# Expert stages begun in the tail of their attention, and keys, values and first queries of three attentions made in the stage before, in a four-layer transformer kernel

## The reference

```python
for i in range(4):
    x = x + attention_i(layernorm(x), ctx)     # a0, a1, a2, a3
    x = x + ffn_i(layernorm(x))                # f0, f1, f2, f3
```

```python
sel = sigmoid(x @ expert_sel.T)                # rows x 16
val, idx = top_k(sel, 4)
val = val / clip(val.sum(-1), 1e-9) * route_scale
out = sum_k val_k * (relu(x @ keys[idx_k]) @ values[idx_k])
```

## Time and profile before

| | us |
|---|---|
| median of 3 runs | 1240.81 (1240.06 to 1242.52) |
| the profiled execution | 1240.38 |
| its span | 1238.6 |
| mean granted TensorE clock, share of full | 0.926 |
| PE busy | 1009.9 (82%) |
| DVE busy | 906.6 (73%) |
| ACT busy | 618.2 (50%) |
| POOL busy | 354.7 (29%) |

### The profile page before, as it was taken

The page is one execution under the profiler, slowest core; times in us unless marked ns, Lnnn a source line. Parts: engine busy times, 40 slices in busy tenths (PEclk is TensorE's granted clock), DMA queues, the critical chain, the costliest instruction groups (busy, mean ns, idle before and its releaser), DMA issues.

```text
span 1238.6 us, 21285 instructions
## 1 busy us (share of the span) xinstructions
PE 1009.9 (82%) x7331; PEld 650.9 (53%) x7331; DVE 906.6 (73%) x2264; ACT 618.2 (50%) x966; POOL 354.7 (29%) x339
## 2 busy tenths in 40 slices
PE   5868700778978996899569999999789879999998
PEld 3653300734546773444227677776545446666665
DVE  4686699777875656778578898885678756666666
ACT  3424576356632335664277777765476423333332
POOL 5600000011210004354198999993111200000000
PEclk9889955789998999999769999999999979999999
DMA  7000000010000000000000000000000000000000
GB/s 272 1 1 1 1 0 0 1 65 1 2 2 1 0 1 1 2 2 2 1 1 2 1 0 0 0 0 1 1 2 2 2 0 10 8 8 8 8 9 18
DMA packets 8956, 13.47 MB, mean 11 GB/s; under 512 B 816, under 2 KB 6704, under 8 KB 8624
## 3 DMA queue, kind: packets, MB, share of 16 engines
q1 hardware_dynamic: 8880, 12.46, 2.9%
HBM read 10.36 MB, written 2.10 MB: 10 GB/s over the span
## 4 chain that ended last, share of the span: by engine, by line
PE 49%; DVE 31%; issue 10%; ACT 6%; POOL 2%; DVEq 1%; DMA 0%; SPq 0%; ACTq 0%; POOLq 0%
DVE big L718 7%; DVE big L713 6%; PE psum L511 5%; PE psum L1895 5%; PE psum L1898 5%; PE psum L1909 5%; DVE big L1802 2%; PE psum L1366 2%; PE psum L1319 2%; PE psum L252 2%; PE psum L1563 2%; PE psum L1328 2%; PE psum L1571 2%; DVE amax L1129 2%; PE psum L465 2%
## 5 line engine op out<-in xcount | busy, mean ns | idle before, releaser
L713 DVE TENSOR_REDUCE big<-psum 128x16 f32<-128x1024 f32 x96 | 114.4, 1221 | 70.4 <-PE psum L465 37.3
L1712 POOL TENSOR_TENSOR big<-big 128x512 f32<-128x512 f32 x128 | 128.7, 1047 | 21.5 <-ACT big L1632 21.5
L1945 ACT ACTIVATE big<-psum 128x512 f32<-128x512 f32 x80 | 47.8, 597 | 142.7 <-PE psum L1895 142.4
L383 POOL TENSOR_TENSOR big<-big,w_const 128x256 f32<-128x256 f32 x48 | 34.7, 724 | 229.4 <-PE psum L511 215.7
L1655 ACT ACTIVATE psum<-big,tmp 128x512 f32<-128x512 f32 x128 | 85.0, 687 | 22.7 <-DVE big L1802 20.0
L1802 DVE SCALAR_TENSOR_TENSOR big<-big,tmp,psum 128x512 f32<-128x512 f32 x128 | 90.4, 744 | 4.8 <-ACT psum L1655 1.9
L718 DVE RECIPROCAL big<-psum 128x256 f32<-128x256 f32 x48 | 84.0, 1750 | 13.4 <-PE psum L511 13.4
L1998 DVE TENSOR_TENSOR big<-big,psum 128x512 f32<-128x512 f32 x80 | 54.5, 687 | 52.6 <-PE psum L1898 52.3
L1909 PEld LDWEIGHTS psum<-tmp,big 128*128 128x128 f32 x512 | 66.7, 191 | 39.9 <-issue 36.3
L619 ACT ACTIVATE big<-psum 128x1024 f32<-128x1024 f32 x64 | 62.0, 1021 | 50.5 <-PE psum L495 50.5
L1328 PE MATMUL psum<-f_downT,tmp 128*128 128x128 f32 x192 | 24.6, 297 | 75.7 <-DVE tmp L1243 75.7
(11 more groups left out here) (241 smaller groups left out, 2319.1 us busy)
## 6 DMA issues: line engine op xcount, KB each, us to landing
out<-X SPq DMA_DIRECT2D x8, 256.0 KB, 2.3
tmp<-in_pack_f SPq DMA_DIRECT2D x1, 1924.0 KB, 7.7
w_f<-in_pack_f SPq DMA_DIRECT2D x1, 1280.0 KB, 12.1
tmp<-in_pack_once SPq DMA_DIRECT2D x1, 960.0 KB, 7.0
X<-in_x SPq DMA_DIRECT2D x1, 768.0 KB, 5.1
w_a<-in_pack_a SPq DMA_DIRECT2D x3, 256.0 KB, 7.5
w_a<-in_pack_a SPq DMA_DIRECT2D x1, 704.0 KB, 9.5
w_f<-in_pack_f SPq DMA_DIRECT2D x1, 576.0 KB, 5.0
```

Source lines behind the costliest of these rows:

```text
L713: dve.tensor_reduce(nm, psum[:, 1 + 2 * t:3 + 2 * t, :].rearrange("p c (r l k) -> p (c r) l k", r=2, k=SK), AX.X, ALU.max, negate=True).th ...
L1712: ins = pool.tensor_tensor(ssum[t][:, h * 512:(h + 1) * 512].rearrange("p (i j) -> p i j", i=ROWS2), st[:, 0, h, 0:ROWS2].unsqueeze(2).to_ ...
```

## The change

1. **Layer norm in parts.** The norms of a1, a2, a3, f1 and f3 are finished in two parts, the first over 16, 20, 20, 24 and 24 tiles. `ln_finish_dve` is split in `ln_var_dve` and `ln_rstd_dve`, and `normalise_act` lets ScalarE normalise a group (four activations).
2. **a1 in f0, a2 in f1, a3 in f2.** K and V of a1 stand ahead of f0's down products, the taking of keys (now eight ScalarE activations with a bias from a new `bk4`), values and keys16 in front of ScalarE's down levels; T, Q, MX and NM of batches 0 and 1 stand between the half groups of f0's groups 5 to 7 and behind them. a2's keys are made in f1's groups 1 to 4, its values in 5 and 6, T(0), Q(0) and Q(1) in 7. a3's all stand in f2's last group. All keys are complete before an attention's loop.
3. **f1 and f3 in the tail of a1 and a3.** T(0) of the expert stage is issued at b = 15, its logits at b = 16, the norm's first part at b = 13 and 14, the gates of group 0 at b = 16. The second part of the norm stands in f1 behind the gates of group 1, and in f3 at its start. f2 is not begun early.
4. **f1's gates** are computed as 1/(1 + exp(-x)): Exp on ScalarE (no table load), then +1 and RECIPROCAL of 128x64 on VectorE. Loops of f1 are unrolled, of f3's TensorE loop the first and last turn.
5. **Memory.** Queries and maxima get a tensor of their own (`hq`), cleared once at the start by GpSimd; the scratch of f1 and f3 moves to the end of `big`, and two buffers of f2 swap places. SyncE's load of f3's weights waits for f0's last down product instead of a1's go. The go semaphores other than f0's are gone.

```diff
...
+        EARLY = 24
+        LN_PARTS = {"a0": ((0, LN0), (LN0, N_TILES)), "f1": ((0, EARLY), (EARLY, N_TILES)),
+                    "f3": ((0, EARLY), (EARLY, N_TILES)), "a1": ((0, 16), (16, N_TILES)),
+                    "a2": ((0, 20), (20, N_TILES)), "a3": ((0, 20), (20, N_TILES))}
...
+        def normalise_act(act, s, g, j, k=0):
+            act.wait_ge(sem(s, "ln"), at(s, "ln") + LN_STEPS * (k + 1))
+            act.wait_ge(sem(s, "normed"), at(s, "normed") + g)
+            act.wait_ge(sem(s, "turned"), at(s, "turned") + g + 1)
+            for t in range(GT):
+                ins = act.activation(hrow[:, j, t * P:(t + 1) * P], tile_of(X, 4 * g + t), ACT.Identity,
+                                     scale=rstd[:, ds(4 * g + t, 1)], bias=shifted[:, ds(4 * g + t, 1)])
+            ins.then_inc(sem(s, "normed"), 1)
...
-            pe.wait_ge(sem(s, "go"), at(s, "go") + 1)
...
+                if b == B and nxt.early:
+                    nxt.logits0(pe)
                 if b >= 2:
                     O(b - 2)
+                if b == B - 1 and nxt.early:
+                    turn(pe, nxt.s, 0, 0, query_taken(L, B))
...
+            if nxt.early:
+                normalise_act(act, nxt.s, 1, 1)
+                take_turned(act, nxt.s, 0, 0)
+                nxt.probs0(act)
...
-                if b == 0:
-                    keys(1)
+                if b == 1:
+                    ln_rstd_dve(dve, s, 1)
                 if 1 <= b <= B:
                     norm(b - 1)
+                if b == B - 2 and early:
+                    ln_rstd_dve(dve, nxt.s, 0)
+                    normalise(dve, nxt.s, 0, 0)
+                if b == B and early:
+                    nxt.gates0(dve)
                 if b >= 2 and b % 2:
                     res((b - 3) // 2)
+                if b == B - 3 and early:
+                    stats_done(dve, s, nxt.s, 0)
+                    ln_var_dve(dve, nxt.s, 0)
...
+                if g == 3:
+                    stats_done(dve, s, "a1", 0)
+                    ln_var_dve(dve, "a1", 0)
+                if g == 4:
+                    ln_rstd_dve(dve, "a1", 0)
+                if g >= 6:
+                    a1.mx(g - 6, 0)
+                    a1.mx(g - 6, 1)
...
+                    if t == 1 and g == 6:
+                        a1.Q(0)
+                    if t == 1 and g == 7:
+                        a1.MX(0, 0)
+                        a1.MX(0, 1)
+                if g == 5:
+                    a1.T(0)
+                if g == 6:
+                    a1.Q(1)
...
+            act.activation(prob1[j], bank(1)[:, 0:GT * MOE1_E], ACT.Exp, scale=-1.0).then_inc(S("f1_ex"), 1)
...
+            dve.tensor_scalar(prob1[j], prob1[j], 1.0, None, ALU.add).then_inc(S("f1_g"), 1)
+            dve.wait_ge(S("f1_g"), 8 * g + 1)
+            dve.reciprocal(prob1[j], prob1[j]).then_inc(S("f1_g"), 1)
...
+                if g == 2:
+                    pe.wait_ge(hs("prep"), 1)
+                    a2.K(0, 6, True)
...
+                if fixed and g == 0:
+                    ln_finish_dve(dve, s, 1)
                 if not (fixed and g >= N_GROUPS - 2):
                     normalise(dve, s, g + 2, j)
...
+                if g == 2:
+                    a2.keys_sin(0, 6)
...
+                    if c == 0 and not one_more:
+                        pe.wait_ge(S("f2_sim"), 4 * N_GROUPS + 2)
+                        pe.wait_ge(S("f2_mw"), 16 * N_GROUPS)
+                        a3.K(0, 0)
+                        a3.K(1, 1)
...
                 for t in range(GT):
                     rows_out(t)
+                    if not one_more and t == 1:
+                        a3.T(0)
+                    if not one_more and t == 2:
+                        a3.Q(0)
```

More of the change, by code:

```diff
@@ L1300, in f0_act @@
                     up_levels(g + 1)
+            act.wait_ge(S("f0_du"), N_GROUPS)
+            for i in range(2):
+                a1.keys(i, (3, 0)[i])
+            for i in range(4):
+                a1.values(i, (1, 2, 4, 5)[i])
+            a1.keys16(0, 0)
+            a1.keys16(0, 1)
             act.wait_ge(S("f0_ego"), 1)
@@ L1343, in build, with f1_logits @@
         hidT1 = [f1.take(512) for _ in range(2)]
-        def f1_pe(pe):
+        def f1_logits(pe, g, j):
+            pe.wait_ge(sem("f1", "hT"), at("f1", "hT") + g + 1)
+            if isinstance(g, int) and g == 0:
+                pe.wait_ge(S("ld_f1"), 16)
+            else:
+                pe.wait_ge(S("f1_ex"), g)
+            for t in range(GT):
+                ins = pe.matmul(bank(1)[:, t * MOE1_E:(t + 1) * MOE1_E], hT[:, j, t * P:(t + 1) * P],
+                                W["f1_sel"], start=True, stop=True)
+            ins.then_inc(S("f1_lg"), 1)
@@ L1358, in f1_pe @@
-            logits(0, 0)
+                f1_logits(pe, g, j)
             def body(g, j, last):
@@ new lines, in body @@
+                if g == 3:
+                    a2.keys16(0)
+                if g == 5:
+                    a2.values(1, 6)
+                    a2.keys16(1)
+                    ln_finish_act(act, "a2", 0)
+                if g == 6:
+                    a2.values(3, 6)
+                    normalise_act(act, "a2", 0, 0)
+            for g in range(N_GROUPS):
+                body(g, g % 2, g == N_GROUPS - 1)
+                if g == 0:
+                    ln_finish_act(act, "f1", 1)
+            a2.rotated16(0)
@@ L1692, in body @@
                     logz(g + 1)
+                if not one_more:
+                    act.preload_act_table_set("natural_log_exp_and_others")
+                    act.wait_ge(S("f2_S"), 4 * N_GROUPS)
+                    act.wait_ge(S("f2_mw"), 16 * N_GROUPS)
+                    for i in range(4):
+                        a3.values(i, i % 2)
+                    a3.keys16(0)
+                    take_turned(act, "a3", 0, 0)
+                    a3.takeQ(0)
+                    a3.takeQ(1)
+                    a3.keys16(1)
+                    take_turned(act, "a3", 1, 1)
+                    a3.takeN(0)
                 for t in range(GT):
@@ L1847, in body @@
                     shift(g + 1)
+                    if not two_more:
+                        stats_done(dve, s, "a3", 0)
+                        ln_var_dve(dve, "a3", 0)
+                else:
+                    normalise(dve, "a3", 0, 0)
+                    a3.keys16(0)
+                    normalise(dve, "a3", 1, 1)
                 for t in range(GT):
@@ L1874, in build, with f3_bank, f3_logits @@
         hid3 = [f3.take(512) for _ in range(2)]
+        def f3_bank(g):
+            return bank(5 if isinstance(g, int) and g == 0 else 7)
+        def f3_logits(pe, g, j):
+            pe.wait_ge(sem("f3", "hT"), at("f3", "hT") + g + 1)
+            if isinstance(g, int) and g == 0:
+                pe.wait_ge(S("ld_f3"), 16)
+            else:
+                pe.wait_ge(S("f3_p"), g)
+            for t in range(GT):
+                ins = pe.matmul(f3_bank(g)[:, t * E3:(t + 1) * E3], hT[:, j, t * P:(t + 1) * P], W["f3_gate"],
+                                start=True, stop=True)
+            ins.then_inc(S("f3_lg"), 1)
```

632 lines of the change are left out of this document (382 added, 250 removed).

## The result

| | before | after |
|---|---|---|
| median | 1240.82 us (17 runs, 1238.25 to 1242.57) | 1236.45 us (17 runs, 1230.41 to 1240.19) |
| profiled execution, its span | 1240.38, 1238.6 | 1236.59, 1234.8 |
| mean granted clock | 0.926 | 0.924 |

The ratio is 0.996, with a 95% interval of 0.9947 to 0.9972: faster, by 3 to 7 us, where 18 were forecast. The time lies outside the range of the prediction. The runs of the change spread over 10 us, and its clock with them: four runs of 1230.4 to 1230.8 had a mean clock of 0.926, the one of 1240.19 had 0.916.

A forecast was written before the change was run, and what follows sets the result against it. The chain lay 49% on TensorE and 31% on VectorE, with the time in the joints between stages. 6.1 + 5.5 − 15.85 + 14.95 + 2.8 + 4.5 = 18.0 us off 1240.4 gave 1222.4, range 1215 to 1229.

The forecast's parts named there:

- its own signs of being wrong: f1's groups over 3 us longer, f1 clock under 0.9 behind group 0, or first batches staying 27, 31, 26 us.
- f0 to a1: Joint before a1: ST(0) near 259.9, 6.0 us gained; with first batches, norm and clock terms, net 6.1 gained.
- First four batches: Score to score in a1, a2, a3: 3.0, 3.25, 1.4 us gained, before norm terms and a1's 2.5 for clock.
- a1 to f1: Joint before f1: first hidden 7.8 us gained, 2.3 lost to half clock on group 0, net 5.5 gained.
- f1's loop: Groups of f1: added keys, values, T, Q, reciprocals and norm steps cost TensorE time, net 15.85 us lost.
- rival C: New waits in f1 drop TensorE to half clock, 10.2 us more per group; four groups give 1263 us; chance 0.04.
- f1 to a2: Joint before a2: 11.8 us left of 23.85, 12.1 gained; first batches 3.25, norm −0.4; net 14.95 gained.
- f2 to a3: Joint before a3: f2's last group 7.5 us longer, head falls to 7.9, first batches 1.4 gained; net 2.8 gained.
- a3 to f3: Joint before f3: first hidden near 1001.8, 6.3 us gained, 1.8 lost to half clock; net 4.5 gained.
- A: Rival: clock stays full through the shorter heads and f1's reciprocals find cover, 1211 us; chance 0.22.
- B: Rival: every f1 group pays 1 us more, TensorE waiting for bank 6; a3's 2.8 not had; 1233 us; chance 0.10.

The follow-up runs named there:

- e3: The change plus unread matmuls filling TensorE's waits in the heads of a1, a2 and a3: 1224.37 us.
- e2: The change with the second part of the attentions' norm moved later on VectorE, behind the maxima (a2, a3) and norm(0): 1222.25 us.
- e4: The change with the edits of e1, e2 and e3 together: 1210.55 us.
- e9: The change plus five unread matmuls in f1 alone, in TensorE's wait behind group 0: 1234.54 us.
- e6: e4 with a2's key products late in f1's groups and f1's hidden buffers released ahead of a1's last residual: 1204.19 us.
- e7: The change without the early start of f1 and f3 in the tails of a1 and a3: 1249.51 us.
- e1: The change with two swaps in VectorE's order in f1 (normalise ahead of gates, half the rotated keys ahead of keys16): 1226.42 us.

## Why the prediction was wrong

It forecast a gain of 18.0 us, and 3.8 came by the profiled executions (4.4 by the medians). Stretch by stretch (the table above), the 14.2 us between them are 10.8 in the first four batches of a1, a2 and a3, 4.1 from a1's ST(4) to f1's last residual and 2.6 in a2's head; all the rest came out 3.3 better. So it named the right joints and got most of their heads right; what failed is the first batches behind them, and two waits in f1. Two of its own signs of being wrong came true: the first batches did not fall below 27, 31 and 26 us, and a window in f1 behind group 0 showed a clock of 0.69.

- **f0 to a1: right.** ST(0) 5.9 us earlier (forecast 6.0), 3.14 us of waiting for T(0) (3.7). The sign given for it, 11 to 12 us from f0's last residual to ST(0), was not: it is 3.99, because the residual itself now stands 7.75 us later (256.06), behind the work put between the last groups.
- **First four batches, "27.36 to 24.3", 31.21 to 27.95, 25.71 to 24.3: the step that failed.** They were taken as the steady batches without the work that moved away, less 0.4 to 0.8 for the norm and 2.5 for the clock in a1 alone: 3.6 gained in all. They lost 7.2 (0.8, 3.0 and 3.4). Of these 10.8 us the half clock is the larger part (e3: 2.9, 3.0 and 3.9 in these batches), the norm's steps the other (e2: 1.3 in a1, 2.1 in a3; in a2 up to 6.7 with the clock). Only a1 of the three attentions was given a term for the clock, by the idle time in front of T(0). The fall came from ST(0) on in a1 (behind 2.46 us of waiting), in a2's head (behind 2.36), and at ST(0) in a3, where no single wait was longer than 1.32. With both causes removed (e4) these batches took 23.93, 27.52 and 23.99, so that the sizes for the work itself were right.
- **a1 to f1: right.** The first hidden is at 370.06 for 382.64, 12.6 earlier, of which 5.1 were brought along from a1's ST(4): 7.5, forecast 7.8, before its 2.3 for half clock on group 0. The half clock came there as forecast: the first four key products take 3.21 us, four of the same form at full clock 1.88 (e9). e6, which takes away this half clock and the wait of 2.96 in front of it, shortens the first group by 4.0. e7 prices both early starts at 13.1.
- **f1's loop: the parts right, two waits dearer.** 0.63 us in front of the middle transposes (forecast 0.6), the reciprocal 0.55 (0.55). But the fourth group took 15.44 in place of 12.3, the key bank's 1.20 behind keys16 and then half clock, which rival C had as a mechanism, at another price; and group 1 ran at 0.69 behind the 2.64. From the first transpose behind group 0 to the last residual it took 90.54 us (382.82 to 473.36) for 72.32 before (391.68 to 464.00), 18.2 more, where the forecast's terms for this stretch are 12.85 (15.85 without the 3.0 of group 0, which lie in front of it): 5.4 too few. The 10.2 us a group that C reckons with are low as well: from residual to residual the groups of the kernel before took mostly 10.6.
- **f1 to a2:** the head 14.3, forecast 11.8; e2 makes it 10.0. The norm steps ahead of the maxima, 1.56 us long, were seen as "norm part" and not as what TensorE waits for.
- **f2 to a3:** last group 30.49 (32.4), head 7.06 (7.9): better by 2.8. f2's group 6, which got Ln, Exp and six steps, took 31.74 for 29.49; that wasn't in the sum, and no run here takes it apart.
- **a3 to f3:** first hidden 5.07 behind the residual (5.5), and from a3's ST(4) to the end 7.2 us were gained for 4.5: the clock there is 1.00, and none of the 1.8 us for it was lost. The trace's 1.28 us for the table load was right: the switch at f3 shows no drain, against the Trainium skill ("ScalarE: Activation LUTs", section "What ACT_TABLE_LOAD costs").

Of the rivals, A's condition (a full clock) is what the experiments made by hand. That e4 then measured A's 1211 is in part luck: it got there by edits that A does not have. The measured time, 1236.45, lies among the values that B was given, up to 1238, but only half by its mechanism. The 2.8 us of a3 were indeed not had: from a2's ST(4) to a3's ST(4) the change is 0.5 us longer. But f1's middle groups took 12.3, little over the 10.9 to 12 of the forecast, and only the fourth waited long for bank 6 (1.20). B's wait in every group shows in e1 (0.86 us in each of four), once the one for normalise is gone. C had the right mechanism, TensorE falling to half clock behind new waits, but was put in f1's middle, where it took one group, and not in the heads.

## What to carry to other kernels

When work in front of a stage is taken away, TensorE has less to do in the joint than before, and new waits can halve its clock (here single waits of 2.36 to 3.14 us and, in a3, three of 0.65 to 1.32 close together were followed by half clock, and filling gave back 3 to 4 us in each attention's first batches): price every new wait of TensorE with the clock behind it. Put small housekeeping steps (here a norm's second part) behind the instruction that the critical engine waits for, even where they are ten times 0.17 us. Where no useful work can fill such a wait, a few matmuls into a free bank can.
